# Moving the transposes of the second layer's W ahead of the attention, in the first turn of a two-layer graph kernel

## The reference

```python
# layer 0: masked attention, 8 heads of 32 (6 static masks, 2 heads masked by adj | eye)
q, k, v = x @ Wq.T + bq, x @ Wk.T + bk, x @ Wv.T + bv
h = layernorm(x + softmax(where(mask, q k^T / sqrt(32), -1e9)) v @ Wo.T + bo)
# layer 1: 4 heads of width 256
Wh = einsum('bni,hoi->bhno', h, W) + bW
e = einsum('bhno,hop->bhnp', Wh, attn)
A = tanh(where(adj, einsum('bhnp,bhmp->bhnm', e, Wh), 0))
hp = relu(einsum('bhnm,bhmo->bhno', A, Wh))            # heads side by side: cat
ha, hf = cat @ A_w.T, h @ fc_w.T
c = sigmoid(hf @ g1_w.T + ha @ g2_w.T + gbias)
out = layernorm(h + hf * c + ha * (1 - c))
```

## Time and profile before

| what | us |
|---|---|
| median of 3 runs | 1093.31 |
| lowest and highest of them | 1091.76, 1093.73 |
| the profiled execution's own time | 1090.47 |
| its span, first to last instruction | 1088.6 |

### The profile page before, as it was taken

How to read it: one execution, slowest core, us unless ns; L and a number is a source line. 1 busy time by engine, 2 the same in 40 slices (tenths; PEclk the granted TensorE clock), 3 DMA queues, 4 the chain that set the end, 5 groups by cost and what they waited for, 6 DMA issues and landing times. The chain is left out here.

```text
span 1088.6 us, 25437 instructions
## 1 busy us (share of the span) xinstructions
PE 1079.7 (99%) x10102; PEld 907.8 (83%) x10102; DVE 704.5 (65%) x1319; ACT 544.6 (50%) x987; POOL 290.2 (27%) x277
## 2 busy tenths in 40 slices
PE   9999999999999999999999999999999999999997
PEld 7888888888888888888888888888788888878887
DVE  7775666657576575766666676575765756666544
ACT  6663544636356273554636456373563735546352
POOL 2533232222332222232232322223322232322200
PEclk9999999999999999999999999999999999999999
DMA  7010001000010000100100010000100100010000
GB/s 264 3 43 19 23 23 40 22 20 19 22 40 22 20 20 21 40 22 23 39 20 19 22 40 22 20 19 22 40 22 20 41 14 26 22 35 9 1 20 20
DMA packets 26589, 32.60 MB, mean 30 GB/s; under 512 B 4160, under 2 KB 23104, under 8 KB 26176
## 3 DMA queue, kind: packets, MB, share of 16 engines
q1 hardware_dynamic: 26128, 31.93, 8.8%
q10 hardware_dynamic: 432, 0.26, 0.1%
HBM read 23.80 MB, written 8.39 MB: 30 GB/s over the span
## 5 line engine op out<-in xcount | busy, mean ns | idle before, releaser
L971 ACT ACTIVATE cat_hi<-bank 128x512 fp32r<-128x512 f32 x128 | 76.6, 598 | 127.2 <-PE bank L394 127.2
L934 ACT ACTIVATE T<-bank 128x512 f32<-128x512 f32 x128 | 75.0, 603 | 86.6 <-PE bank L394 86.6
L1106 DVE SCALAR_TENSOR_TENSOR cat_lo<-bank,cat_hi 128x512 fp32r<-128x512 f32 x128 | 86.6, 686 | 39.1 <-ACT cat_hi L971 37.0
L389 PE MATMUL bank<-hT_hi,g_lo 128*128 128x512 f32 x256 | 102.7, 401 | 0.0
L382 PE MATMUL bank<-cat_hi,aw_lo 128*128 128x512 f32 (+1 forms) x272 | 102.4, 377 | 0.0
L381 PE MATMUL bank<-cat_lo,aw_hi 128*128 128x512 f32 (+1 forms) x272 | 102.4, 377 | 0.0
L383 PE MATMUL bank<-cat_hi,aw_hi 128*128 128x512 f32 (+1 forms) x272 | 102.4, 377 | 0.0
L1473 POOL TENSOR_TENSOR probs<-probs,den 128x512 f32<-128x512 f32 x64 | 67.5, 1057 | 124.0 <-DVE den L1198 122.9
L390 PE MATMUL bank<-U_hi,wt_hi 128*128 128x512 f32 x256 | 99.9, 390 | 0.0
L389 PE MATMUL bank<-U_hi,wt_lo 128*128 128x512 f32 x256 | 99.8, 390 | 0.0
L390 PE MATMUL bank<-hT_hi,g_hi 128*128 128x512 f32 x256 | 99.8, 390 | 0.0
(11 more groups left out here) (199 smaller groups left out, 2751.5 us busy)
## 6 DMA issues: line engine op xcount, KB each, us to landing
y<-in_x SPq DMA_DIRECT2D x16, 512.0 KB, 3.5
out<-res SPq DMA_DIRECT2D x15, 512.0 KB, 3.0
x_raw<-in_xT SPq DMA_DIRECT2D x14, 512.0 KB, 3.3
W_nat<-in_Wn SPq DMA_DIRECT2D x1, 1028.0 KB, 7.6
adjS_u<-in_adjS SPq DMA_DIRECT2D x16, 64.0 KB, 3.0
attn_nat<-in_attn SPq DMA_DIRECT2D x1, 1024.0 KB, 8.6
raw_A<-in_AwT SPq DMA_DIRECT2D x1, 1024.0 KB, 9.2
x_second<-in_xT SPq DMA_DIRECT2D x1, 512.0 KB, 11.1
```

The source lines that it names most:

```text
L389: pe.matmul(out, wsel(w[1]), dsel(d[0]), start=first and n == 0, stop=False)
L934: take(act.activation(T[:, n % DC, n // DC, :], bank[:], ACT.Copy), "B", f"T{n}", g)
L971: act.activation(cat_hi[:, n, :], bank[:], ACT.Relu).then_inc(cat_hi_ready, 1)
L1106: return dve.scalar_tensor_tensor(out=out, in0=bank, scalar=bias, in1=hi.bitcast(F32), op0=op, op1=ALU.subtract)
```

## The change

In turn 0 the four transposed tiles W0 to W3 and their splits move. On PE `W_transposed` stood behind the last product for G and now stands behind the fourth, in front of `attention`. On ACT `W_high` stood behind the last `G_high` and now stands in front of `x_split(1)` and `attention(0)`. On DVE `W_low` stood in two pieces around `new_h(0)` and is now one piece in front of `attention(0)`. The bank list and the order of `set_hi` follow. No instruction is added or taken away, and no transfer is moved in SP's order.

```diff
-SPLIT_ORDER = ("G0", "G1", "G2", "G3", "G4", "G5", "G6", "G7", "W0", "W1", "W2", "W3", "FC")
+SPLIT_ORDER = ("G0", "G1", "G2", "G3", "W0", "W1", "W2", "W3", "G4", "G5", "G6", "G7", "FC")
...
-               "probT0:5 probT1:0 G0:1 G1:2 probT2:7 G2:3 probT3:4 G3:6 attn0:5 attn1:0 G4:1 G5:2 G6:3 y0:4 y1:7 "
-               "G7:6 W0:1 W1:2 W2:3 W3:5 q0:0 q1:4 FC:6 FF:7 hT0:1 hT1:2 k0:3 k1:5")
+               "probT0:5 probT1:0 G0:1 G1:2 probT2:7 G2:3 probT3:4 G3:6 W0:1 W1:2 W2:7 W3:3 attn0:5 attn1:0 G4:4 G5:6 G6:1 "
+               "y0:2 y1:7 G7:3 q0:0 q1:4 FC:6 FF:7 hT0:1 hT1:2 k0:3 k1:5")
...
 # TensorE
                     G_products(range(3, 4))
+                    W_transposed()
                     attention(0, range(DC))
                     G_products(range(4, 7))
                     project(0)
                     G_products(range(7, H2 * DC))
-                    W_transposed()
                     queries(1)
...
 # ScalarE
                     G_high(range(3, 4))
+                    W_high()
                     x_split(1, x_second)
                     attention(0)
...
                     G_high(range(7, H2 * DC))
-                    W_high()
                     queries(1)
...
 # VectorE
                     G_low(range(4))
+                    W_low(range(4))
                     attention(0)
                     G_low(range(4, 7))
                     residual(0)
                     G_low(range(7, H2 * DC))
-                    W_low(range(2))
                     new_h(0)
-                    W_low(range(2, 4))
                     h_T(0)
```

## The result

Over 22 executions of each kernel in turn, the changed one took 1094.41 us in the median (1090.44 to 1095.35) and the kernel before 1092.09 (1089.21 to 1094.05). The ratio is 1.0023, with a 95% interval of 1.0014 to 1.0032: about +2.5 us. The change makes the kernel slower beyond the noise; whether by more than the 0.2% that I had set as a boundary, the interval leaves open. The times of both kernels spread over 5 us in clusters, and half of what follows is about why. The profiled execution of the changed kernel took 1092.26 us with a span of 1090.4, against 1090.47 and 1088.6.

A forecast was written before the change was run, and what follows sets the result against it. PE was taken as the bound, a queue of matmuls hiding the other engines. Work 0, first stop +0.23 and second stop +0.85 sum to +1.1 us: 1093.31 + 1.1 = 1094.4 us, range 1092.0 to 1096.5.

The forecast's parts named there:

- The transposes on PE, at nothing: PE, turn 0: W's transposes move from behind G7 to before attention, -1.67 and +1.67 us, banks free: zero.
- ACT, at_hi 1.83 to 2.06 later: ACT, turn 0: four high parts of W now precede x_hi and at_hi, delaying at_hi by about 1.9 us.
- The first stop: PE at `project`, waiting for at_lo: 1.9 us later, 1.67 us earlier, so +0.23 us at `queries(1)`.
- the hidden wait: PE's wait for at_lo in front of `project`, unseen in the profile: 0.24 us before, forecast to grow to 0.54.
- The second stop: PE at `h_T`, waiting for `new_h`: 0.85 us of new wait, `h_T` starting 1.08 us later.
- rigid: Chain from at_hi through at_lo, `project`, `residual`, statistics and roots to `new_h`: all of it 1.9 us later.
- the slack: Time to spare between `new_h`'s arrival and `h_T` on PE before the change: 0.82 us.
- Behind h_T: PE from `h_T` to T0: hT_lo and T0 move by the same amount, no new wait, no time given back.
- B: Rival: idle PE at `h_T` halves the clock until T0, +4.7 us with the stop, 1098.0 us; chance 0.04.
- C: Rival: issue pauses in written-out code come or go, 1.0 us each; beside the sum, chance 0.08.
- the loop's turns change in length: Sign that the prediction is wrong; it expected equal distances between equal points of later turns, as before.
- the clock shows less than 1.00 after `h_T`: Sign that the prediction is wrong; it expected the 0.85 us wait at `h_T` to leave PE's clock unchanged.

The follow-up runs named there:

- at_first: Changed kernel with ACT's copies of the attention in front of x_split instead of behind it; ratio to the kernel before 1.0019.
- half: Against the kernel before, only W0 and W1 moved in front of the attention, W2 and W3 left behind G7; ratio 1.0011.
- filler: Changed kernel with 8 useless transposes added on PE in front of FF's products; ratio to the kernel before 1.0005.
- after2: Changed kernel run and profiled again without an edit; profiled execution 1095.38 us, ratio to the kernel before 1.0031.
- after_count: Changed kernel with 16 semaphore instructions, no matmul, added on PE in front of FF's products; ratio to the kernel before 0.9999.

## Why the prediction was right, and where it was not

The direction was right, and the range held the time. That the median of 1094.41 us falls on the forecast of 1094.4 is luck: over 22 executions the kernel before has a median of 1092.09 and not the 1093.31 of its three, and the difference is 2.3 us by the medians where +1.1 was forecast. The two errors cancel. The chance was too small on the right side: I gave 0.84 to "within 0.2%" and 0.11 to slower by more, and it came out at 0.23%.

- *The transposes on PE, at nothing.* Nearly. No bank was waited for, and G3 to W is 0.87 us where G7 to W was 0.86. But from W to the attention it is 30.77 - 28.93 = 1.84 us, not 1.67.
- *ACT, at_hi 1.83 to 2.06 later.* +1.85. But that the attention "is not what ends last" was wrong. It is later by 1.84 us on PE, for the reason just given, and at_first shows its end level with ACT's queue.
- *The first stop.* `project` +1.88 against 1.9. PE came later than forecast by the same 0.17 us, so the hidden wait is 0.34 by starts (35.25 - 32.18 - 2.73) and not 0.54; the profile names 0.21. At `queries(1)` +0.03 instead of +0.23: its first matmul follows G7's start by 0.67 us where W's followed by 0.86.
- *The second stop.* +1.29 at h_T instead of +1.08, by two errors of opposite sign. The chain was longer than "rigid": DVE paused 0.28 us for issue in the middle of the statistics, and the roots and `new_h` came at +2.31 instead of +1.9. And the slack was 1.02 us, not 0.82: the way over from `new_h` to h_T, put at 0.25, is 0.05 (45.12 - 43.69 - 1.38), and 0.05 or 0.06 in the five other profiles in which h_T had to wait as well. 2.31 - 1.02 is 1.29. That the transposes were the filler was read rightly (half: +0.29; filler: 0.87 us of free work). The pause of DVE, 0.21 to 0.29 us, is in all seven profiles that have low parts of W in front of the attention and in none of the other seven; its cause was not isolated.
- *Behind h_T.* T0 +1.36 against the sum of +1.1, inside the bounds of 0.86 to 1.6. The shortest executions agree: 1090.44 against 1089.21, +1.2.
- *Rivals B and C, the term that was mis-sized.* Pauses for issue stood in the sum with nothing, "the shift does not depend on what makes them differ", and in C with 1.0 us at a chance of 0.08. In after2 the pause in the scores at 50 us and the clock behind it cost 3.6 us. Such executions are what I hold for the step of the ratio from some 1.0012, the stops alone, to 1.0023; the share that each execution owes to them was not measured, since only one was profiled. Of the 22 executions of the changed kernel ten show a mean clock of 0.997 or 0.998, and all ten lie between 1094.17 and 1095.30; three others above 1094.3 do not show it, and filler and after_count show 0.998 in three executions each without being long, so the mean clock alone is a weak sign.
- *The clock.* B had 0.04. As it was put, it did not come: behind the stop at h_T, 0.98 us by the profile, the clock stays 1.00, as its "against" said. But the clock did fall some 9 us later, at 53.5 us, behind a pause that no rival had there, and "the loop's turns change in length" and "the clock shows less than 1.00 after `h_T`" were my own signs of being wrong. What the Trainium skill says ("TensorE: Matmul & The Clock Gate", Part 1: The HAM clock gate) agrees with after2 and half: the level fell behind a long pause and came back with work. Length alone does not decide it: the longer pauses of 2.07 and 2.10 us in the attention left the clock at 1.00.

What stays open: the executions above 1093 us of the kernel before itself (9 of 22) were not caught in a profile. A fall of the clock seems to belong to them too: with its executions beside the other runs there are 140 of this kernel whose mean clock is on record, and all 23 with 0.997 or less lie above 1092.5. The pause in the attention left the clock at 1.00 in both of its long cases, and their executions took 1091.93 and 1091.22 us; so it fits the executions between 1091 and 1092 better than the longest ones. If the change takes that pause away, as no profile with W in front shows it, the two kernels trade one risk for another, and 1.0023 is the stops and the difference of the two.

## What to carry to other kernels

On an engine that is full, moving work costs nothing by itself; ask what it was hiding. Work that stands between a producer's request and its answer is cover; the price of moving it away is what the answer comes later by, less the slack. And a stream of very short instructions that crosses a block of the program is a place where an execution can lose 1 to 4 us or nothing: shift it by a few instructions before believing a difference of 0.2%.

## What the runs showed of the hardware

PE paused for issue 0.39 to 2.10 us in runs of 128 matmuls 11 ns apart, always after the same count for one order (113 in the scores behind T0, 117 or 109 in the first loop turn, 110 in the last but one, 96 in the attention), in some executions of a kernel and not in others. In all 14 cases it went on 2.3 to 2.9 us behind a 16 KB instruction transfer. Around the pauses of 1.58 and 1.67 us the granted clock showed 0.79 and 0.86 over windows of 5 us (50 to 55 us), and 0.50 in the half microseconds from 53.0 to 56.0 and from 54.0 to 57.0; behind the pauses of 0.39 to 1.07 us in the scores, and behind those of 0.80, 2.07 and 2.10 in the attention, it showed 1.00.
